# Attention's output centred by its weights in a two-layer language-model tower on one core, and sequence 0's transposes behind the read

## The reference, cut to what matters

```
h = tok(x)                                  # embedding, convolution, relu, projection
h = h + rnn2(norm(h))                       # two recurrent layers, 1024 steps, 8 sequences at once
h = h + routed_ffn(norm(h))                 # the best 511 tokens of each sequence
n = norm(h)                                 # second norm
retrieved = phasor memory read with n       # per sequence, cumulative over tokens
normed = (retrieved - mean) / sqrt(var + 1e-5) * ln_w + ln_b
h = h + normed @ Wo + bo                    # attention's output
n = norm(h)                                 # third norm: (h - mean(h)) / sqrt(var(h) + 1e-5)
h = h + experts(n)                          # 8 experts of width 128, the best 2 by softmaxed gates
```

## Time and profile before

| | us |
|---|---|
| median of 3 runs (lowest, highest) | 1123.51 (1123.03, 1123.75) |
| the profiled execution, its own time | 1123.85 |
| its span, first to last instruction | 1122.0 |
| PE busy | 1061.1 (95%) |
| ACT busy | 769.2 (69%) |
| DVE busy | 686.4 (61%) |
| POOL busy | 147.4 (13%) |
| mean granted clock of PE | 0.968 |

### The profile page before, as it was taken

The page is one execution under the profiler, slowest core; times in us unless marked ns, Lnnn a source line. Parts: engine busy times, 40 slices in busy tenths (PEclk is TensorE's granted clock), DMA queues, the critical chain, the costliest instruction groups (busy, mean ns, idle before and its releaser), DMA issues.

```text
span 1122.0 us, 62678 instructions
## 1 busy us (share of the span) xinstructions
PE 1061.1 (95%) x26978; PEld 859.2 (77%) x26978; DVE 686.4 (61%) x3132; ACT 769.2 (69%) x4585; POOL 147.4 (13%) x220
## 2 busy tenths in 40 slices
PE   4799999999999999999999999999899879889998
PEld 2688899999999999999999999999744368833332
DVE  7566455555555555555555544444456758899996
ACT  1466677777767777777777776666567888667664
POOL 4300000011000100000110000000003402341320
PEclk9699999999999999999999999898699989999999
DMA  5000000000000000000000000000000000167786
GB/s 147 7 10 9 9 9 15 9 10 9 9 11 13 9 9 9 10 14 9 9 5 5 4 5 5 5 4 5 3 1 1 1 2 1 29 240 249 277 294 209
DMA packets 30642, 47.29 MB, mean 42 GB/s; under 512 B 12298, under 2 KB 21651, under 8 KB 30364
## 3 DMA queue, kind: packets, MB, share of 16 engines
q1 hardware_dynamic: 29820, 43.15, 11.5%
q10 hardware_dynamic: 544, 0.13, 0.1%
HBM read 40.88 MB, written 2.39 MB: 39 GB/s over the span
## 4 chain that ended last, share of the span: by engine, by line
PE 80%; DVE 9%; ACT 5%; issue 3%; DMA 2%; POOL 1%; SPq 0%; DVEq 0%; ACTq 0%; POOLq 0%
PE bank L680 44%; PE bank L777 7%; PE bank L671 5%; PE bank L760 4%; PE bank L441 3%; PE bank L540 2%; PE bank L1750 2%; PE bank L1696 2%; DMA space<-weights_kept 1%; PE bank L1437 1%; PE bank L1470 1%; PE bank L755 1%; DVE space L2159 1%; PE bank L1619 1%; PE bank L772 1%
## 5 line engine op out<-in xcount | busy, mean ns | idle before, releaser
L680 PE MATMUL bank<-space,whh_hi 128*128 128x32 f16 (+1 forms) x16384 | 574.0, 175 | 8.3 <-DVE space L808 4.4
L680 PEld LDWEIGHTS bank<-space,whh_hi 128*128 128x128 f16 x16384 | 481.9, 96 | 71.1 <-DVE space L808 8.0
L808 DVE TENSOR_TENSOR space<-h_f,space 128x16 f16<-128x16 f32 x2048 | 284.6, 176 | 365.5 <-ACT h_f L789 360.9
L789 ACT ACTIVATE h_f<-bank 128x16 f32<-128x16 f32 x2048 | 293.4, 184 | 226.4 <-PE bank L680 220.3
L795 ACT ACTIVATE space<-bank 128x16 f16<-128x16 f32 x2048 | 292.6, 184 | 1.1 <-PE bank L680 1.1
L671 PE MATMUL bank<-space,whh_lo 128*128 128x32 f16 (+1 forms) x2096 | 131.4, 177 | 0.0
L777 PE MATMUL bank<-space,wih_hi 128*128 128x32 f16 x2048 | 129.1, 177 | 0.0
L760 PE MATMUL bank<-xr,wih_hi 128*128 128x32 f16 x512 | 97.4, 190 | 0.0
L441 PE MATMUL bank<-onehot,tab 128*128 128x128 f16 x448 | 95.5, 219 | 0.5 <-DVE prepare_cur L491 0.5
L755 PE MATMUL bank<-ones,bias 128*128 128x32 bf16 x512 | 91.7, 179 | 0.0
L671 PEld LDWEIGHTS bank<-space,whh_lo 128*128 128x128 f16 x2096 | 90.1, 96 | 0.0
(11 more groups left out here) (309 smaller groups left out, 1598.9 us busy)
## 6 DMA issues: line engine op xcount, KB each, us to landing
space<-weights_kept SPq DMA_DIRECT2D x64, 512.0 KB, 7.8
space<-in_x SPq DMA_DIRECT2D x28, 129.0 KB, 3.1
out<-res SPq DMA_DIRECT2D x7, 256.0 KB, 9.8
space<-in_wrec SPq DMA_DIRECT2D x1, 768.0 KB, 4.3
space<-in_wx SPq DMA_DIRECT2D x1, 744.5 KB, 8.9
weights_kept<-wturned SPq DMA_DIRECT2D x8, 36.0 KB
whole<-weights_kept SPq DMA_DIRECT2D x8, 36.0 KB
brec<-in_brec SPq DMA_DIRECT2D x1, 260.0 KB
```

Source lines behind the costliest of these rows:

```text
L680: mm = pe.matmul(own[:, m, 0:copies, :], w[:, k, m * P:(m + 1) * P], state[:, k, :].unsqueeze(1).to_broadcast([P, copies, B]), start=False ...
L789: act.activation(h_f[layer][:, s % 2, :, :], own, ACT.Tanh, scale=scale[layer]).then_inc(s_h[layer], 1)
L808: dve.tensor_tensor(h[layer][:, :, s % RINGS[layer], 1, :], h_f[layer][:, s % 2, :, :], h[layer][:, :, s % RINGS[layer], 0, :], ALU.subtra ...
```

## The change

The output weights are centred on the chip once (the mean over the 64 outputs taken from each row) and get a 65th column with their sums; `add_out` then adds 65 columns, so that `res` stays centred with its sum beside it. The third norm needs no mean and no centring: `third_square` and `third_scale` read `res`. The four products of `project_out` are 130 columns wide and lie across the end of bank 6 and the start of bank 7, over the last columns of the place where weights are transposed. Sequence 0's side products wait for `add_out`'s reading of that place (s_wor) and stand behind `read(b)`. `third_square(y + 2)` goes from step 2 to step 1.

```diff
-        wobd = sb("wobd", [P, P])
+        wobd = sb("wobd", [P, 2, D + 1])
+        wsum = sb("wsum", [P, 1])
...
+        def centred_weights(dve, link, i):
+            rows = slice((i + 1) % 2 * D, ((i + 1) % 2 + 1) * D)
+            own = wobd[rows, (i + 1) % 2, :]
+            if i == 0:
+                link(dve.reduce_sum(wsum[:, :], wobd[:, :, 0:D], AX.XY))
+            elif i < 3:
+                link(dve.scalar_tensor_tensor(own[:, 0:D], wsum[rows, :].to_broadcast([D, D]), -1.0 / D, own[:, 0:D],
+                                              ALU.mult, ALU.add))
+            else:
+                link(dve.tensor_copy(own[:, D:D + 1], wsum[rows, :]))
...
             elif k == 3 and o < 20 and o % 10 != 5:
                 wide_weights(dve, link, o - (o > 5) - (o > 15))
+            elif k == 3 and 20 <= o < 25:
+                centred_weights(dve, link, o - 20)
...
-        cwb = lo2[:, 2200:2200 + D]
+        cwb = lo2[:, 2200:2200 + D + 1]
+        att_out = banks[3][:, 252:252 + TT * (D + 1)]
...
             def third_square(x):
                 act.wait_ge(s_xc, B + x + 1)
-                act.activation(sq[:, :, :], xc[:, :, :], ACT.Square, scale=D ** -0.5).then_inc(s_sq, 1)
+                act.wait_ge(s_var, B + x)
+                act.activation(sq[:, :, :], res[:, span(x), 0:D], ACT.Square, scale=D ** -0.5).then_inc(s_sq, 1)
...
                 if step == 1 and y + 1 < B:
                     third_copy(y + 1, bank[3])
-                elif step == 2 and y + 2 < B:
-                    third_square(y + 2)
+                    if y + 2 < B:
+                        third_square(y + 2)
...
-                    mm = pe.matmul(bank[7][:, i * P:(i + 1) * P], ntb[:, i * P:(i + 1) * P], wobd[:, :],
+                    mm = pe.matmul(att_out[:, i * 2 * (D + 1):(i + 1) * 2 * (D + 1)], ntb[:, i * P:(i + 1) * P],
+                                   wobd[:, :, :].rearrange("p h d -> p (h d)"),
...
+                read(b)
                 if b == 4:
-                    pe.wait_ge(s_sd, b)
+                    pe.wait_ge(s_wor, b)
                     third_turn(pe, bank[6], 0)
                 elif b == 5:
-                    pe.wait_ge(s_sd, b)
+                    pe.wait_ge(s_wor, b)
                     gates(0, bank[6][:, D:2 * D])
-                read(b)
-                if b == 6:
-                    pe.wait_ge(s_sd, b)
+                elif b == 6:
+                    pe.wait_ge(s_wor, b)
                     weights_turned(0, bank[6][0:(NE + 1) * TT, P:2 * P])
...
             def add_out(b):
-                own, part = res[:, span(b), 0:D], tmp8[:, :, 0:D]
+                own, part = res[:, span(b), :], tmp8[:, :, :]
...
-                link(dve.tensor_tensor(own, own, part, ALU.add))
+                dve.tensor_tensor(own, own, part, ALU.add).then_inc(s_xc, 1)
...
             dve.wait_ge(s_row_k, 1)
+            link(dve.reduce_sum(stat[:, 0, 0:1], cwb[:, 0:D], AX.X))
+            link(dve.scalar_tensor_tensor(cwb[:, 0:D], stat[:, 0, 0:1].to_broadcast([P, D]), -1.0 / D, cwb[:, 0:D], ALU.mult,
+                                          ALU.add))
+            link(dve.tensor_tensor(cwb[:, D:D + 1], cwb[:, D:D + 1], stat[:, 0, 0:1], ALU.add))
             for b in range(B):
...
-                if b == 1:
-                    third_mean(0)
-                    third_centre(0)
-                elif b == 2:
+                if b == 2:
                     third_variance(0)
                 elif b == 3:
                     third_scale(0)
-                    third_mean(1)
-                elif b == 4:
-                    third_centre(1)
...
-                elif b == 7:
-                    third_mean(2)
-                    third_centre(2)
...
                 if y + 2 < B:
-                    if step == 0:
-                        third_mean(y + 2)
-                    elif step == 1:
-                        third_centre(y + 2)
-                    elif step == 5:
+                    if step == 5:
                         third_scale(y + 2)
```

More of the change, by code:

```diff
@@ L1262, in _ @@
             act.wait_ge(s_row_b, 1)
-            act.activation(cwb[:, :], bank[6][:, D:2 * D], ACT.Copy).then_inc(s_row_k, 1)
+            act.activation(cwb[:, :], bank[6][:, D:2 * D + 1], ACT.Copy).then_inc(s_row_k, 1)
             for b in range(2):
@@ L1668, in _ @@
             pe.matmul(bank[6][:, D:2 * D], ones[:, :], bias[:, B_O:B_O + D], start=True, stop=False, skip_group_check=True)
-            pe.matmul(bank[6][:, D:2 * D], lnb[0:D, :], wobd[0:D, 0:D], start=False, stop=True,
+            pe.matmul(bank[6][:, D:2 * D + 1], lnb[0:D, :], wobd[0:D, 0, :], start=False, stop=True,
                       skip_group_check=True).then_inc(s_row_b, 1)
@@ L2046, in add_out @@
             def add_out(b):
-                own, part = res[:, span(b), 0:D], tmp8[:, :, 0:D]
-                link(dve.tensor_tensor(own, own, rows(cwb[:, :]), ALU.add))
+                own, part = res[:, span(b), :], tmp8[:, :, :]
+                link(dve.tensor_tensor(own, own, cwb.unsqueeze(1).to_broadcast([P, TT, D + 1]), ALU.add))
                 dve.wait_ge(s_rs, b + 1)
-                dve.tensor_tensor(part, tokens(bank[7][:, :]), spread(stat[:, 7, :]), ALU.mult).then_inc(s_wor, 1)
+                dve.tensor_tensor(part, tokens(att_out), stat[:, 7, :].unsqueeze(2).to_broadcast([P, TT, D + 1]),
+                                  ALU.mult).then_inc(s_wor, 1)
                 dve.wait_ge(s_wor, b + 1)
-                link(dve.tensor_tensor(own, own, part, ALU.add))
+                dve.tensor_tensor(own, own, part, ALU.add).then_inc(s_xc, 1)
             dve.tensor_scalar(lnb[:, :], ones32[:, :], column(LN_B), None, ALU.mult).then_inc(s_lnb, 1)
             per = lambda x: x.unsqueeze(2).to_broadcast([P, TT, NE])
-            def third_mean(x):
-                link(dve.reduce_sum(stat[:, 0, :], res[:, span(x), 0:D], AX.X))
-            def third_centre(x):
-                dve.wait_ge(s_nrm, B + x)
-                dve.scalar_tensor_tensor(xc[:, :, :], spread(stat[:, 0, :]), -1.0 / D, res[:, span(x), 0:D], ALU.mult,
-                                         ALU.add).then_inc(s_xc, 1)
             def third_variance(x):
@@ L2071, in third_scale @@
                 dve.wait_ge(s_xs, OPEN + B + x)
-                dve.tensor_tensor(nrm[:, :, :], xc[:, :, :], spread(stat[:, 4, :]), ALU.mult).then_inc(s_nrm, 1)
+                dve.tensor_tensor(nrm[:, :, :], res[:, span(x), 0:D], spread(stat[:, 4, :]), ALU.mult).then_inc(s_nrm, 1)
             def third_low(x):
@@ L2237, in lay_out @@
     col[:, 9] = np.tile(f("L0_ffn_b2"), 2)
-    wkq2, wobd = z(P, P), z(P, P)
+    wkq2, wobd = z(P, P), z(P, 2, D + 1)
     wkq2[:D, :D], wkq2[D:, D:] = f("L1_attn_Wk2"), f("L1_attn_Wq2")
-    wobd[:D, :D] = wobd[D:, D:] = f("L1_attn_Wo")
+    wobd[:D, 0, :D] = wobd[D:, 1, :D] = f("L1_attn_Wo")
     eb2 = z(P, D)
```

4 lines of the change are left out of this document (2 added, 2 removed).

## The result

| | before | after |
|---|---|---|
| median, us (lowest, highest; runs) | 1122.9 (1122.12, 1123.75; 6) | 1130.8 (1126.54, 1134.1; 6) |
| ratio of medians, 95% interval | | 1.0065 [1.0051, 1.008] |
| the profiled execution, its span | 1123.85, 1122.0 | 1133.7, 1131.9 |

The six runs lie unevenly: two at 1126.6, one at 1128.6, three from 1133.0 to 1134.1. The profiled one is of the upper group, so its trace shows what those lose; what the lower ones have is read from experiments.

The account below looks back on a forecast made before the run. PE was taken as the bound, in a ring with ACT in the read and full in the experts; 1123.85 + 0.75 + 4.1 - 1.6 = 1127.1, against the median 1126.8 us, range 1124.5 to 1129.8.

Parts of the forecast that it names:

- PE's clock: Attention's read: new PE gaps are shorter and less empty than the 902 us stop, so clock falls count 0.
- the sum: Whole kernel: profiled 1123.85 plus 0.75 plus 4.1 minus 1.6 gives 1127.1, or 1126.8 against the median.
- Rival A: Attention's read: clock falls in the new gap, adding 1 to 3.5 us, so 1128 to 1130.3; chance 0.22.
- weights' transpose: Read, behind read(6): waits for s_wor at 6, starting near 980.2; delay 4.1 us at `memory(7)`, after 3.7 at `project_out(5)`.
- main term, +4.1 for the moves: Attention's read: sequence 0's transposes, gates and weights' transpose moved behind reads cost 4.1 us together, bounds -0.9 and 5.2.
- Five operations in the recurrence, 0: Recurrence: five DVE operations on centred weights and column sums, covered by PE's work, cost 0; at most 1.4 us.
- Three operations on `cwb`, +0.75: Before the loop over sequences: three linked DVE operations delay `rounded(2)` and PE's scores by 0.75 us, bounds 0 and 1.1.
- Transposes behind `read(4)`, +4.25 at `attention_kept(4)`: Read: transposes wait for DVE's multiplication in `add_out(3)`; ACT's queued copy and cosines make `attention_kept(4)` 4.25 us later.
- C and D: Read: C, late wait absorbed, 1123.7 to 1125.3, chance 0.14; D, wait already met when PE arrives, 1121.7, chance 0.04.
- Gates: Read, behind `read(5)`: 0.38 us leaves the ring, so the delay is 3.9 us at `attention_kept(5)`.
- No mean, no centring, -1.6: Experts: ACT's square no longer waits for centring, saving 0.41 us in each of four sequences; read 0; bounds 0 and -2.5.
- Rival B: Experts: DVE sets the pace, each sequence shortens by 1.37 us, five times, giving 1121.5; chance 0.06.

Follow-up runs that it names:

- experiment 6: Kernel before, with the three side products moved behind the read but keeping the old wait s_sd: 1125.3 us, ratio 1.0027.
- experiment 14: Changed kernel with the operations on `cwb` ahead of masked(0) and filler matmuls in the two long PE gaps: 1126.06 us, ratio 1.0026 to the kernel before.
- experiment 9: Changed kernel with filler matmuls on PE in all four stretches that the moves empty: 1126.81 us, ratio 1.0031 to the kernel before.
- experiment 12: Changed kernel with side products in bank 0 in their old places, operations on `cwb` left where the change put them: 1122.69 us, ratio 0.9993 to the kernel before.
- Experiment 5: Kernel before, with only sequence 0's transposes moved behind the read and waiting for s_wor: 1127.74 us, ratio 1.0049.
- experiment 13: Changed kernel with ACT's third_copy(0) behind key_sines(6) and fillers in the two long PE gaps: 1124.8 us, ratio 1.0012 to the kernel before.
- experiment 11: Kernel before, with only gates and weights' transpose moved behind the read and waiting for s_wor: 1123.1 us, ratio 1.0008.
- experiment 3: Changed kernel with the moves undone, 128-column products in bank 7, attention's 65th column left out: 1122.24 us, ratio 0.9986 to the kernel before.
- experiment 7: Changed kernel with side products in bank 0 in their old places and operations on `cwb` ahead of masked(0): 1119.4 us, ratio 0.9979 to the kernel before.
- experiment 2: Kernel before, with only the three moves behind the read, waiting for s_wor: 1133.53 us, ratio 1.0091.
- experiments 4: Changed kernel with 11 filler matmuls behind read(4) and 5 behind read(6): 1127.11 us, ratio 1.0039 to the kernel before without one outlying run.
- experiment 8: Changed kernel with side products in bank 0, `cwb` operations ahead of masked(0), and 20 filler matmuls before keys(0): 1117.84 us, ratio 0.9962 to the kernel before.

## Why the prediction failed

The side was right, slower, with the mechanism named; the size was not, and the median lies 1.0 us above the range.

**The step that failed** is in "PE's clock": "That stop was longer and emptier than the new ones, so the sum has 0 for it." Both halves were true of the rows, and the conclusion did not follow from them: the earlier trace rows show one stop that was enough, and nothing on how little is enough. The clock fell after a wait of 2.76 us among thin matmuls, and in experiment 6 with no wait above 1.34 us. It did so twice in the profiled run, and for the 0 of the sum the two falls took about 7 us. **Rival A** named the cause and the first place and put it at 1128 to 1130.3; it had one fall, and no second one before the experts. The profiled execution has both, +2.41 at `attention_kept(5)` (the sum expected -0.35 there) and +3.92 +0.83 after `attention_kept(6)` (it expected about +0.2 from the weights' transpose). A chance of 0.22 was too low for something that the kernel had already done at 902, and the range ended short of two falls.

The trace of before had more to say against the step. In the last part of the recurrence its clock falls several times between 704 and 800 us, and there PE was hardly idle by its modelled busy time, in which only short stalls can hide:

```profile
704.00:708.00 4.00, 3.99 (x134) 3.78 (x131) 2.07 (x14) 3.13 (x25) 0.96 (x2) 0.65 0.02 4
708.00:712.00 4.00, 4.00 (x132) 3.86 (x129) 1.83 (x13) 3.06 (x24) 0.00 (x0) 0.50 0.01 4
```

So the clock had already fallen without an empty stretch like that of 902.

The Trainium skill (TensorE: Matmul & The Clock Gate, section "A second HAM failure mode: psum-queue depth-cycling") states that short pauses between groups of matmuls, frequent enough, make the clock swing between its levels. Experiment 6, with 1.34 us as its longest wait, fits that in so far as its pauses are short; it has one fall and no swinging, so it does not show the page's case. The prediction weighed only the section on long waits.

**What the sum is worth without the falls.** Its main term, +4.1 for the moves, was right to half a microsecond: the table above has +4.07 for this part of the kernel where no fall disturbs it (experiment 14; +4.06 in experiment 9), 4.56 less a gain of 0.5 that the sum had as 0. Experiment 14, which has no fall in the read and the operations on `cwb` early, cost +2.9 us by the ratio, where the sum without those operations has 4.1 - 1.6 = 2.5. Other agreements of the total are in part luck. Two of the six runs gave 1126.54 and 1126.69, the sum's 1126.8; that they had no falls after 950 is an inference, since no trace of them exists (their mean clock, 0.967 each, is above the profiled run's 0.956). And experiment 9 cost +3.5 for +3.25, but its trace holds a fall at the scores of sequence 2, 1.6 us that the sum does not have, and an experts' part shorter by 2.3 us and not 1.6, which nearly pay for each other.

Term by term:

- *Five operations in the recurrence, 0.* They cost 0.35 us. DVE's instructions of L808 (L821 in the changed kernel), one for each step and layer, mark the time: up to the 129th all traces agree (51.89 to 52.00 us after the first), and at the 193rd the five traces without the five operations have 75.68 to 75.77, the eleven with them 76.03 to 76.16. An idle share of DVE was no full cover.
- *Three operations on `cwb`, +0.75.* From the first of them (L2125, 916.94) to `rounded(2)` (917.64) 0.70 us pass; the scores of sequence 2 lost 0.71 on those of sequence 1. What the step missed is that with this delay the clock can fall at these scores too, in six of eight traces (experiment 12), and then the way to the scores of sequence 3 takes 0.5 to 1.6 us more; in the profiled run of the changed kernel it did not. Why the delay brings the fall no run shows.
- *Transposes behind `read(4)`, +4.25 at `attention_kept(4)`.* Measured +4.13: PE's wait for L2068, the copy, the cosines, in this order. The sign of C and D, `attention_kept(4)` within a us of the read's end, did not come, and both fell with it. Experiment 5 shows that this move is the costly one (5.5 us with its fall), experiment 13 that 1.6 to 2.1 us of the loss were the copy's place in ACT's queue, a second fault beside PE's own wait.
- *Gates, -0.38, and weights' transpose, +0.2.* Together too small to be measured by the medians (experiment 11: between -0.3 and +2.1 us); in its trace the stretch up to `attention_kept(7)` is 0.6 us longer.
- *No mean, no centring, -1.6.* The mechanism held: ACT's square (L1289) waits for nothing now, and a sequence is shorter. But the cycle went to 16.00 us, not 16.14, which the sum took for what is left without the wait; PE was idle for 0.09 of that 16.14, and why the rest went too is not shown. It makes about 0.55 for each of four sequences, -2.4 from sequence 0 to 5. And the read, where the sum had 0, gave 0.5 us: 29.6 for 30.09 in the table above, in experiments 3, 7 and 12 alike. Experiment 3's -1.6 agrees with the forecast's only by chance, since it nets these two gains against the 0.35 of the recurrence, the operations on `cwb` and the fall at the scores of sequence 2. *Rival B* fell: PE is busy for 16.00 of 16.00 us, DVE for 15.38, so PE sets the pace and DVE's microsecond buys nothing in the experts.

So the whole: moves +10.2 (experiment 2), centring -1.6 (experiment 3), +8.6 against 7.3 measured for both; taken out of the change instead, the moves are worth 8.1 (experiment 12). The difference would fit the changed kernel's short runs, if these had no falls: experiment 2 has no such run in four. Only one run of each has a trace, so this is an inference, and why one kernel should lose the time in every run and the other in most is open.

What stays open too is where the runs between 1126.7 and 1133 lose their time, since only one run of a kernel has a trace. Experiment 6 shows the gap between the two: its profiled run has one fall and lies 1.9 us above the kernel before, its median 3.

**Why the moves were there at all:** the 130-column products lie across two banks, over the place of sequence 0's side products, which must then wait for DVE's reading. The layout made the wait, and another bank took it away: experiment 12 keeps everything else of the change and is 8.1 us faster than the change as made, by the two ratios, which is level with the kernel before. With the operations on `cwb` early as well (experiment 7) the gain of the centring shows, 2.4 us on the kernel before.

## What to carry to other kernels

A wait in front of PE in a stretch where its work is already thin is to be priced twice: the delay itself, and then all serial PE work behind it at half clock, with the cases of one and of two falls both in the range. Moving work behind a product has a price even without a wait, if another engine's copy stands early in its queue (experiment 6). Before moving work behind a new semaphore, ask which buffer makes the semaphore necessary, and look for a bank that is free at that time; and look at what the consumer's copy holds up in its own engine's queue. Where a gap can't be closed, matmuls into an unread bank can keep the clock, as long as they end before the ring needs PE; they did not always (experiments 4 and 13). And compare two traces by intervals from a common event, not by their absolute times: `attention_kept(4)` of experiment 6 stands at 956.81, ahead of the 957.07 of before, and is 1.3 us late all the same.

## What the runs showed of the hardware

- The clock fell after a stretch with no wait over 1.34 us, PE busy for 2.66 of 4 us in it (experiment 6), and in the recurrence of the kernel before with PE busy for 7.99 of 8 us (704 to 712). In other places it held through stretches as thin as that of experiment 6: the kernel before has 2.80 of 4 at 924 to 928 with 1.00 and the changed one 2.81 with 1.00, while experiment 9, with 2.81 there too, has 0.80. No bound can be read from these; in nearly the same code it fell once and held twice, and the same code after the read held in experiment 7 and fell in 8 (976 to 980). The times of the changed kernel spread wider than before's: 7.6 us over six runs, 1.6 over six of the one before.
- At half clock the scores took 3.55 us for 2.05 and `project_out`'s products 2.07 for 1.11. Filler ahead of the attention bought 1.6 us by the medians (experiment 8 against 7, whose intervals overlap a little).
